# Turning x by a transfer, one state scaled by TensorE through diagonal matrices, and a new layout of the small stages

## The chip, the cores and the metric

The kernel runs on one core of a Trainium2 chip. The metric is the device time of one execution in microseconds (us), lower is better. TensorE is PE in the views, VectorE is DVE, ScalarE is ACT, GpSimd is POOL, SyncE is SP. PEld stands for TensorE's weight loads.

## The reference

32 sequences of 750 positions and 256 channels pass through three blocks. Cut to what is computed:

```python
# block 1: every second position, in segments of 128 positions
scores = einsum('bsqd,bskd->bsqk', x, x) / sqrt(256)
h = einsum('bsqk,bskd->bsqd', softmax(scores), x)
# block 2: h = h + mamba(layernorm(h))
x_in, z = split(xn @ W_in.T)                # 512 and 512 channels
u  = silu(conv4(x_in) + b_conv)
dt = softplus(u @ W_dt.T + b_dt); Bm = u @ W_B.T; Cm = u @ W_C.T   # 16 states
state = exp(dt * A) * state + (dt * u) * Bm ; y = sum over states of state * Cm
h = h + (y * silu(z)) @ W_out.T
# block 3: h = h + experts(layernorm(h)): 64 experts, the best 8 of each token,
#          256 places in each expert, silu(x Wg) * (x Wu) @ Wd, weighted and added
```

All of it is in float32.

## The kernel before

**Three phases.** The sequence phase works through blocks 1 and 2 and the routing of block 3, one sequence after the other. Then a short phase counts tokens by expert, and the expert phase gathers, multiplies and scatters. The change touches the sequence phase alone.

**A sequence's sixteen states.** Tokens of a sequence are 3 segments of 128. The recurrence runs state by state, `k` from 0 to 15, over 512 channels (4 chunks of 128 partitions) times 384 tokens. For each state the engines do this:

- ScalarE multiplies `dtu_t` (dt * u, tokens on the partitions) by the state's column of B in three operations (`scaled_dbu`, L380, into one of two buffers `dbu_t`), and makes `decay` with four exponentials (`decays`, L392, four buffers). It works two states ahead.
- TensorE turns `dbu_t` into `psB` with twelve transposes, in two pieces of 4 and 8 (`turn_dbu`, L932). `psB` exists once: a piece is overwritten when the scan of the state before has read it.
- VectorE runs the recurrence as two scans (`scan_piece`, L621), first 512 elements, then 1024, and signals `s_go` with a small instruction (L616).
- GpSimd multiplies by C (`times_c`, L360), when the next state's scan has begun.
- TensorE turns that product and adds it up in `psY`, three states later (`sum_y`, L944).

**The small stages.** All else of the sequence phase is cut into steps that are spread over the sixteen states, in the gaps around the recurrence: `body` of each engine lists at `if k == ...` what it does in a state. While sequence `b` is scanned, sequence `a = b + 2` is in its attention and first norm (`early`), `n = b + 1` in its projections, convolution, softplus and B and C (`front`), `m = b - 1` in its gate and output projection (`back`), `o = b - 2` in its second norm (`late`), and `c = b - 3` in its routing (`routed`). In a state TensorE does the first piece of `turn_dbu`, then `sum_y`, then the second piece, then its small stages. VectorE does its small stages first and then the two scans. ScalarE does a part of its small stages ahead of `scaled_dbu`, most between it and `decays`, and a few behind.

**Two banks.** The results of the small stages pass through two PSUM banks, `psM0` and `psM1`. `SLOTTED` names the products of each bank in the order in which they take it, and `LAG` says of which sequence each is at that time; a product can start when the one before it in its bank has been read. The names: `QT0`, `QT1` x turned, `S` the scores, `PT` probabilities turned, `AT0`, `AT1` the attention's output, `XN0`, `XN1` the normed input turned, `X0` to `X3` and `Z0` to `Z2` the input projections, `D0` to `D3` dt, `CB` B and C, `BT` B turned, `DU0` to `DU2` dt * u turned, `YT0` to `YT2` the gated y turned, `O0`, `O1` the output projection, `X2T0`, `X2T1` the second norm turned, `LG` the router's logits.

**Queues.** SP issues all transfers of this phase in a fixed order, each behind its wait: it stores a finished sequence, loads x (`load_x`, two transfers), stores and loads h, passes B and C through DRAM and spreads C over the partitions in four groups, and stores the routing.

**Carriers.** Where an instruction waits at a place that could also be reached with a register's value, the program before adds an increment of a semaphore `s_turn` that nobody reads; the wait then sits in a separate semaphore instruction ahead of the operation. On VectorE that holds for each first scan, for the aggregation of the norms' statistics (L653), and for the routing's MAX8 (L781, L803) and MATCH_REPLACE8 (L788, L816).

## Time and profile before

| | |
|---|---|
| median of 3 executions | 3411.68 us |
| lowest of the three | 3406.43 us |
| the profiled execution's own time | 3408.89 us |
| its span, first to last instruction | 3407.0 us |
| mean granted TensorE clock | 0.96 of full speed |
| busy over the span | TensorE 87%, VectorE 84%, ScalarE 83%, GpSimd 62% |
| first scan of a sequence begins | 71.31 us |

The third execution, at 6037.72 us, is far from the other two; the median is one of the two near ones. A profile shows one execution. Busy time counts an instruction from its start to its end, and neighbours on an engine overlap by up to a tenth of a microsecond, so what a step takes on an engine is better read from start to start. "Idle before" is the time in which the engine had nothing running, and the name behind it is who ended that. The steady part, from about 110 to 2760 us, repeats with each sequence.

### The profile page before, as it was taken

The page shows a single profiled execution, that of the slowest core. Times are in us where ns is not written, and L with a number is a line of the kernel's source. Part 1 is how long each engine was busy: PE and PEld are TensorE (multiplying, and loading weights), DVE is VectorE, ACT ScalarE, POOL GpSimd, SP SyncE. Part 2 cuts the span into 40 slices and gives each one's busy share as a digit, 9 for nine tenths or more (in the row PEclk, how much of TensorE's full clock was granted, in tenths as well). Part 3 has the DMA queues.
Part 4 walks back from the last instruction along what each step waited for, and adds up shares of the span by engine and source line. Part 5 has one row for each costly group of instructions (what it writes and reads, how often), then busy time and mean ns, then how long its engine had stood idle before and what let it go on. Part 6 is the DMA issues. An engine that isn't in the chain of part 4 may idle for free. (4 is left out here: it accounts for less than half of the span.)

```text
span 3407.0 us, 56637 instructions
## 1 busy us (share of the span) xinstructions
PE 2969.6 (87%) x19009; PEld 2397.3 (70%) x19009; DVE 2858.1 (84%) x4628; ACT 2823.4 (83%) x5457; POOL 2105.5 (62%) x780
## 2 busy tenths in 40 slices
PE   6899999999999999999999999999999987566664
PEld 4677777777777777777777777777777776455543
DVE  4888999999999999999999999999999997444442
ACT  5999999999999999999999999999999996211110
POOL 0666666666666666666666666666666665177776
PEclk8999999999999999999999999999999998588887
DMA  2111121212112111122222212112221111377774
GB/s 94 52 52 52 55 63 63 63 63 63 58 60 63 56 52 58 63 63 63 63 63 63 64 63 63 59 59 63 63 63 63 59 54 32 94 151 147 149 149 82
DMA packets 187455, 240.52 MB, mean 71 GB/s; under 512 B 45152, under 2 KB 165440, under 8 KB 187200
## 3 DMA queue, kind: packets, MB, share of 16 engines
q1 hardware_dynamic: 162624, 199.44, 18.7%
q0 software_dynamic: 24576, 37.77, 6.6%
q8 instruction: 149, 2.44, 0.3%
q14 instruction: 106, 0.87, 0.1%
HBM read 176.07 MB, written 61.08 MB: 70 GB/s over the span
## 5 line engine op out<-in xcount | busy, mean ns | idle before, releaser
L360 POOL TENSOR_TENSOR hid<-hid,c_all 128x1536 f32<-128x1536 f32 x512 | 1770.4, 3458 | 1100.4 <-DVEq L616 1094.9
L621 DVE TENSOR_TENSOR_SCAN hid<-decay,hid,psB 128x1024 f32<-128x1024 f32 x512 | 1201.4, 2347 | 88.7 <-PE psB L932 42.4
L392 ACT ACTIVATE decay<-dt,a_neg 128x383 f32<-128x383 f32 x2048 | 1086.4, 606 | 0.4
L380 ACT ACTIVATE dbu_t<-dtu_t,b_t 128x512 f32<-128x512 f32 x1536 | 993.2, 714 | 7.5 <-PE psB L932 7.4
L932 PE MATMUL psB<-ident,dbu_t 128*128 128x128 f32 x6144 | 856.5, 276 | 108.4 <-DVE hid L621 102.7
L932 PEld LDWEIGHTS psB<-ident,dbu_t 128*128 128x128 f32 x6144 | 699.0, 141 | 248.5 <-issue 122.7
L944 PE MATMUL psY<-ident,hid 128*128 128x128 f32 x6144 | 757.1, 273 | 1.7 <-POOL hid L360 1.7
L944 PEld LDWEIGHTS psY<-ident,hid 128*128 128x128 f32 x6144 | 689.7, 141 | 2.0 <-POOL hid L360 1.9
L621 DVE TENSOR_TENSOR_SCAN hid<-decay,psB 128x512 f32<-128x512 f32 x512 | 623.3, 1217 | 15.5 <-PE psB L932 10.7
L1019 PE MATMUL psM<-u,w_dt 128*128 128x384 f32 x1024 | 353.2, 488 | 3.4 <-ACT u L424 2.7
L1434 ACT ACTIVATE e_side<-e_psL,e_in_tile 128x128 f32<-128x128 f32 x128 | 45.8, 363 | 260.1 <-DVE e_in_tile L1558 259.4
L1019 PEld LDWEIGHTS psM<-u,w_dt 128*128 128x128 f32 x1024 | 185.0, 191 | 106.8 <-ACT u L424 2.9
L1407 POOL DMA_INDIRECT out_dram<-e_ys,e_dst_st x128 | 205.2, 1603 | 70.4 <-issue 59.3
L1009 PE MATMUL psM<-w_in,turned 128*128 128x512 f32 x384 | 181.4, 609 | 43.2 <-ACT zs_t L419 42.3
L721 DVE SCALAR_TENSOR_TENSOR u<-xin,w_cv,u 128x384 f32<-128x384 f32 x384 | 208.2, 610 | 8.4 <-ACT xin L412 7.2
L1001 PE MATMUL psM<-turned,w_in 128*128 128x384 f32 x512 | 183.2, 491 | 2.0 <-ACT xin L412 1.3
L1058 PE MATMUL psM<-w_out,yz 128*128 128x256 f32 x768 | 179.0, 384 | 0.7 <-issue 0.7
L1520 DVE COPY e_xt<-e_psG 128x512 f32<-128x512 f32 x64 | 44.3, 692 | 158.5 <-PE e_psG L1460 158.5
L1460 PE MATMUL e_psG<-e_ident,e_xg 128*128 128x128 f32 x256 | 50.6, 330 | 134.5 <-DMA e_xg<-x_weights_dram,e_src_st 134.3
L1398 POOL DMA_INDIRECT e_xg<-x_weights_dram,e_src_st x128 | 127.8, 998 | 49.2 <-issue 37.8
L1058 PEld LDWEIGHTS psM<-w_out,yz 128*128 128x128 f32 x768 | 143.0, 193 | 18.5 <-issue 1.1
L1009 PEld LDWEIGHTS psM<-w_in,turned 128*128 128x128 f32 x384 | 68.4, 191 | 114.0 <-issue 61.7
(148 smaller groups left out, 3294.3 us busy)
## 6 DMA issues: line engine op xcount, KB each, us to landing
c_all<-bc_rows_dram SPq DMA_DIRECT2D x128, 768.0 KB, 4.8
out_dram<-h SPq DMA_DIRECT2D x64, 384.0 KB, 5.6
h<-out_dram SPq DMA_DIRECT2D x32, 384.0 KB, 3.6
x_weights_dram<-normed SPq DMA_DIRECT2D x32, 384.0 KB, 2.6
xs<-in_x_dram SPq DMA_DIRECT2D x32, 256.0 KB
e_wg<-in_gate_dram SPq DMA_DIRECT2D x64, 128.0 KB, 2.7
e_wu<-in_up_dram SPq DMA_DIRECT2D x64, 128.0 KB, 3.0
e_wd<-in_down_dram SPq DMA_DIRECT2D x64, 128.0 KB, 3.4
```

The costliest lines, as they stand in the source:

```text
L360: nc.gpsimd.tensor_tensor(hid[k % 4][:, :, :], hid[k % 4][:, :, :], c_all[:, k, :].unsqueeze(1).to_broadcast([P, CH, L]), ALU.mult).then_i ...
L380: last = nc.scalar.activation(dbu_t[k % 2][:, t, :], dtu_t[q][:, t, :], ACT.Copy, scale=b_t[q][:, t, k:k + 1])
L392: last = nc.scalar.activation(decay[k % 4][:, c, 1:L], dt[q][:, c, 1:L], ACT.Exp, scale=a_neg[:, c, k:k + 1])
L621: nc.vector.tensor_tensor_scan(h[:, lo:hi], flat(decay[k % 4])[:, lo:hi], flat(psB)[:, lo:hi], h[:, lo - 1:lo] if j else 0.0, ALU.mult, AL ...
L721: last = nc.vector.scalar_tensor_tensor(out=u[:, c, :], in0=xin[:, c, t:t + L], scalar=w_cv[:, c, t:t + 1], in1=u[:, c, :], op0=ALU.mult, ...
L932: last = nc.tensor.transpose(flat(psB)[:, i * P:(i + 1) * P], dbu_t[k % 2][:, t, c * P:(c + 1) * P], ident[:, :])
L944: last = nc.tensor.matmul(psY[:, t, c * P:(c + 1) * P], hid[k % 4][:, c, t * P:(t + 1) * P], ident[:, :], is_transpose=True, start=(k == 0 ...
L1001: last = nc.tensor.matmul(psM[slot(name)][:, 0:L], w_in[:, k, c * P:(c + 1) * P], turned[:, k, :], start=(k == 0), stop=(k == KD - 1))
L1009: last = nc.tensor.matmul(psM[slot(name)][:, :], turned[:, k, t * P:(t + 1) * P], w_in[:, k, DI:2 * DI], start=(k == 0), stop=(k == KD - 1))
L1019: last = nc.tensor.matmul(psM[slot(name)][:, 0:L], w_dt[:, k, c * P:(c + 1) * P], u[:, k, :], start=(k == 0), stop=(k == CH - 1))
L1058: last = nc.tensor.matmul(psM[slot(name)][:, i * D:(i + 1) * D], yz[:, c, s * P:(s + 1) * P], w_out[:, c, :], start=(c == 0), stop=(c == C ...
L1407: nc.gpsimd.indirect_dma_start(out=h_out, out_offset=bass.IndirectOffsetOnAxis(ap=dst_st[q][:, h:h + 1], axis=0), in_=ys[q % 4][:, h, :], ...
```

## The change

**x turned by a transfer.** The host hands over a second, already turned copy of every second row of x, and `load_x` gets a third transfer, `xt`. The products `QT0` and `QT1` and their copies are gone; `scores` reads `xt`. The scale 1/16 was put into the copies as a factor of 1/4 on each side; now the exponential applies it, and the row's maximum is scaled by a second VectorE instruction.

**State 11 by diagonal matrices.** `DIAG` was empty and now holds 11. ScalarE skips `scaled_dbu` in that state. VectorE makes three 128x128 diagonal matrices of B's column in one operation (`spread_b`), and `turn_dbu` multiplies `dtu_t` by them, in place of turning `dbu_t`.

**Steps and banks.** The small stages stand in other states, and the products in another order and other banks. `XN1` is copied by ScalarE, no longer by VectorE. The increments of `s_turn` are gone. The loop over sequences on GpSimd is written out.

```diff
-DIAG = ()
+DIAG = (11,)
-SLOTTED = (("X0", "X2", "Z0", "Z2", "D0", "D1", "D2", "X2T0", "D3", "CB", "AT0", "YT0", "DU1", "O0", "XN1"),
-           ("O1", "X1", "X3", "Z1", "LG", "QT0", "QT1", "S", "PT", "X2T1", "BT", "AT1", "YT1", "DU0", "YT2",
-            "DU2", "XN0"))
+SLOTTED = (("X2T1", "X0", "X2", "Z0", "Z2", "D0", "YT0", "S", "PT", "AT0", "YT1", "DU0", "DU2", "XN0", "O1"),
+           ("XN1", "X1", "X3", "Z1", "LG", "D1", "X2T0", "D2", "D3", "CB", "AT1", "BT", "YT2", "DU1", "O0"))
...
             def load_x(a):
...
+                sp.dma_start(xt[:, :, 0:(S + DIL - 1) // DIL],
+                             w["x_t"][a].rearrange("(k p) t -> p k t", p=P)).then_inc(s_x, 16)
...
-            with pool.Fori(0, NB) as b:
+            for b in range(NB):
...
                     last = nc.scalar.activation(prob[:, s, :], psM[slot("S")][:, s * P:(s + 1) * P], ACT.Exp,
-                                                bias=nmax[:, s:s + 1],
+                                                bias=nmax[:, s:s + 1], scale=D ** -0.5,
...
             def row_max(a):
                 filled("S", a)
-                nc.vector.tensor_reduce(nmax[:, :], psM[slot("S")][:, 0:L].rearrange("p (s k) -> p s k", s=NSEG),
-                                        AX.X, ALU.max, negate=True).then_inc(s_nm, 1)
+                nc.vector.tensor_reduce(rmax[:, :], psM[slot("S")][:, 0:L].rearrange("p (s k) -> p s k", s=NSEG),
+                                        AX.X, ALU.max).then_inc(s_rm, 1)
+                dve.wait_ge(s_rm, a + 1)
+                nc.vector.tensor_scalar(nmax[:, :], rmax[:, :], -(D ** -0.5), None, ALU.mult).then_inc(s_nm, 1)
...
+            def spread_b(n, r):
+
+                dve.wait_ge(s_out[slot("BT")], number("BT", n))
+                for i, k in enumerate(DIAG):
+                    last = nc.vector.tensor_tensor(diag[:, i, :, :], ident[:, :].unsqueeze(1).to_broadcast([P, NSEG, P]),
+                                                   b_t[r][:, :, k:k + 1].to_broadcast([P, NSEG, P]), ALU.mult)
+                last.then_inc(s_dg, 1)
...
             def scores(b):
-                for name in last_of("QT0", "QT1"):
-                    copied(name, b)
+                pe.wait_ge(s_x, 48 * (b + 1))
                 emptied("S", b)
                 for s in range(NSEG):
                     for kd in range(KD):
-                        t = turned[:, kd, s * P:(s + 1) * P]
+                        t = xt[:, kd, s * P:(s + 1) * P]
```

The small stages by state, where they moved (TensorE: `D2` from state 7 to 8, `D3` from 8 to 9, `CB` from 9 to 10, `O1` from the next sequence's state 0 to 15, `X0`, `X1` and `X3` one state later, `Z0` and `Z1` from 3 to 4, `DU2` from 14 to 13, `YT0` from 11 to 6, `YT2` from 13 to 12, `BT` from 10 to between the pieces of 12, `XN1` from 15 to state 0 of the next, `X2T1` from 9 to state 0 one sequence later; VectorE: the routing's operations, before in states 6 to 9 with most of them in 7, over states 5 to 10, `finish_dt` of the first half from 9 to 10, its second half and both halves of `drive` from 10 to 11, the norm's statistics of h1 from 12 to 13, `norm` of h1 from 15 to 14).

TensorE, states 9 to 12 of a sequence, before. `xs` is x, `yz_t` the gated y, `bc_rows` B and C, `u` holds dt * u by then, and a number behind a name is its buffer.

```order
L932 MATMUL psB<-ident,dbu_t1 128x128 x8
L1028 MATMUL psM0<-u,w_bc 32x384 x4
L953 MATMUL psM1<-ident,normed2 128x128 x3
L932 MATMUL psB<-ident,dbu_t0 128x128 x4
L944 MATMUL psY<-ident,hid3 128x128 x12
L932 MATMUL psB<-ident,dbu_t0 128x128 x8
L1036 MATMUL psM1<-ident,bc_rows 128x128 x3
L988 MATMUL psM0<-xs,normed1 128x256 x2
L988 MATMUL psM1<-xs,normed1 128x256
L932 MATMUL psB<-ident,dbu_t1 128x128 x4
L944 MATMUL psY<-ident,hid0 128x128 x12
L932 MATMUL psB<-ident,dbu_t1 128x128 x8
```

And after the change, from the small stages of state 10 on:

```order
L1022 MATMUL psM1<-u,w_bc 32x384 x4
L982 MATMUL psM0<-xs,normed1 128x256 x2
L982 MATMUL psM1<-xs,normed1 128x256
L928 MATMUL psB<-diag,dtu_t1 128x128 x4
L943 MATMUL psY<-ident,hid0 128x128 x12
L928 MATMUL psB<-diag,dtu_t1 128x128 x8
L952 MATMUL psM0<-ident,yz_t 128x128 x4
L931 MATMUL psB<-ident,dbu_t0 128x128 x4
L943 MATMUL psY<-ident,hid1 128x128 x12
L1030 MATMUL psM1<-ident,bc_rows 128x128 x3
L931 MATMUL psB<-ident,dbu_t0 128x128 x8
```

The product of B and C (`u,w_bc`) moved one state back, in front of the attention's output and of the diagonal products of state 11.

ScalarE from state 9 to 11 before. `soft` is softplus, `normed1` holds the turned probabilities here.

```order
L430 ACTIVATE xin<-psM0,b_dt 128x384
L465 ACTIVATE normed1<-psM1 128x384
L438 ACTIVATE soft<-xin 128x768
L440 ACTIVATE soft<-soft 128x768
L442 ACTIVATE soft<-soft 128x768
L392 ACTIVATE decay2<-dt1,a_neg 128x383 x4
L380 ACTIVATE dbu_t1<-dtu_t1,b_t1 128x512 x3
L403 ACTIVATE turned2<-psM1 128x384
L447 ACTIVATE bc_rows<-psM0 32x384
L392 ACTIVATE decay3<-dt1,a_neg 128x383 x4
```

And now:

```order
L421 ACTIVATE xin<-psM1,b_dt 128x384
L456 ACTIVATE normed1<-psM0 128x384
L429 ACTIVATE soft<-xin 128x768
L431 ACTIVATE soft<-soft 128x768
L433 ACTIVATE soft<-soft 128x768
L438 ACTIVATE bc_rows<-psM1 32x384
L385 ACTIVATE decay3<-dt1,a_neg 128x383 x4
L373 ACTIVATE dbu_t0<-dtu_t1,b_t1 128x512 x3
```

The three scalings into `dbu_t1` of state 11 and the copy into `turned2` are no longer there, and the copy into `bc_rows` stands in ScalarE's state 9, while the product that it waits for stands in TensorE's state 10.

## Rows read from the trace of the kernel before

**Rows 1.** Windows: busy us of each engine, count, granted clock, DMA share, GB/s.
```profile
1000.00:1880.00 880.00, 821.90 (x5540) 668.35 (x5538) 832.22 (x1221) 853.59 (x1600) 552.56 (x161) 1.00 0.20 61
```
**Rows 2.** Waits of VectorE from 1000 to 1880 us: total us, times, longest.
```profile
DVE hid L621 <- PE psB L932: 9.8, 20, 0.7
DVE mv L653 <- DVE stat L648: 3.0, 20, 0.2
DVE nmax L643 <- PE psM L979: 2.5, 9, 0.3
...
DVE gleft L788 <- DVE gtop L784: 1.9, 10, 0.5
DVE top L803 <- DVE masked L797: 1.5, 10, 0.2
...
DVE hid L621 <- ACT decay L392: 0.4, 1, 0.4
```
**Rows 3.** Waits of ScalarE, same window; the longest of its three.
```profile
ACT denom L491 <- PE psM L1068: 10.4, 10, 1.0
```
**Rows 4.** Groups by line, 1000 to 1880 us: count, busy us, mean ns, idle before.
```profile
L380 ACT ACTIVATE dbu_t<-dtu_t,b_t 128x512 f32<-128x512 f32 x480 | 310.4, 714 | 0.0
...
L621 DVE TENSOR_TENSOR_SCAN hid<-decay,psB 128x512 f32<-128x512 f32 x160 | 194.8, 1217 | 1.1 <-issue 0.6 <-ACT decay L392 0.4
...
L403 ACT ACTIVATE turned<-psM 128x384 f32<-128x384 f32 x40 | 18.9, 472 | 0.0
...
L630 DVE COPY turned<-psM 128x384 f32<-128x384 f32 x20 | 10.0, 539 | 0.0
...
L751 DVE TENSOR_TENSOR biased<-score,bias 128x192 f32<-128x192 f32 x10 | 3.3, 334 | 0.0
...
L829 DVE TENSOR_SCALAR wsum<-wsum 128x3 f32<-128x3 f32 x10 | 1.7, 169 | 0.3
```
**Rows 5.** Timeline of states 13 to 15: start us, us, engine, line, count.
```profile
1551.24 1.22 DVE L621 TENSOR_TENSOR_SCAN hid<-decay,psB 128x512 f32<-128x512 f32 x1
...
1552.56 2.35 DVE L621 TENSOR_TENSOR_SCAN hid<-decay,hid,psB 128x1024 f32<-128x1024 f32 x1
...
1553.17 0.60 PE L932 MATMUL psB<-ident,dbu_t 128*128 128x128 f32 x4
...
1553.61 1.47 PE L944 MATMUL psY<-ident,hid 128*128 128x128 f32 x12
...
1554.83 1.22 DVE L621 TENSOR_TENSOR_SCAN hid<-decay,psB 128x512 f32<-128x512 f32 x1
...
1554.96 1.09 PE L932 MATMUL psB<-ident,dbu_t 128*128 128x128 f32 x8
...
1555.89 0.60 PE L953 MATMUL psM<-ident,u 128*128 128x128 f32 x4
...
1556.33 3.62 PE L1058 MATMUL psM<-w_out,yz 128*128 128x256 f32 x16
...
1559.79 0.60 PE L932 MATMUL psB<-ident,dbu_t 128*128 128x128 f32 x4
...
1561.02 1.22 DVE L621 TENSOR_TENSOR_SCAN hid<-decay,psB 128x512 f32<-128x512 f32 x1 [0.28 <-issue]
```
**Rows 6.** Timeline of VectorE, state 6.
```profile
1512.82 2.35 DVE L621 TENSOR_TENSOR_SCAN hid<-decay,hid,psB 128x1024 f32<-128x1024 f32 x1 [0.30 <-PE psB L932]
```
**Rows 7.** Timeline of TensorE, state 5 of the next sequence.
```profile
1595.09 0.49 PE L953 MATMUL psM<-ident,xs 128*128 128x128 f32 x3
...
1598.00 0.60 PE L932 MATMUL psB<-ident,dbu_t 128*128 128x128 f32 x4
```
**Rows 8.** Timeline of TensorE, the scores in state 7.
```profile
1522.13 1.50 PE L979 MATMUL psM<-turned 128*128 128x128 f32 x12
```
**Rows 9.** Timeline of TensorE at the start of the run.
```profile
5.58 0.87 PE L953 MATMUL psM<-ident,xs 128*128 128x128 f32 x3 [5.58 <-DMA xs<-in_x_dram]
...
8.74 2.90 PE L979 MATMUL psM<-turned 128*128 128x128 f32 x12 [0.67 <-ACT turned L403]
```

More of the change, by code:

```diff
@@ L214, in number @@
             ahead = [LAG[o] - LAG[name] + (i <= at) for i, o in enumerate(names)]
-            if not isinstance(batch, int):
-                return batch * len(names) + sum(ahead)
             return sum(min(max(batch + a, 0), NB) for a in ahead)
@@ L224, in each @@
         def each(eng, body):
-            def one(b, q):
-                fixed = isinstance(b, int)
-                body(b, q, scans=not fixed or 0 <= b < NB, back=not fixed or 0 <= b - 1 < NB,
-                     late=not fixed or 0 <= b - 2 < NB, routed=not fixed or 0 <= b - 3 < NB,
-                     front=not fixed or 0 <= b + 1 < NB, early=not fixed or 0 <= b + 2 < NB)
             for b in range(-2, NB + 3):
-                one(b, b % 2)
+                body(b, b % 2, scans=0 <= b < NB, back=0 <= b - 1 < NB, late=0 <= b - 2 < NB,
+                     routed=0 <= b - 3 < NB, front=0 <= b + 1 < NB, early=0 <= b + 2 < NB)
         block = ctx.enter_context(nc.Block())
@@ L241, in wait @@
                 after(sp, sem, count)
-                if not isinstance(count, int):
-                    sp.sem_inc(s_turn, 1)
             def load_x(a):
@@ L506, in body @@
                 for k in range(NS):
-                    if isinstance(b, int) and b == -1 and k == 0:
+                    if b == -1 and k == 0:
                         negated_a()
@@ L580, in body @@
                             copy_yz(m, 1)
-                    if k == 12:
                         if front:
-                            copy_dtu(n, r, 0)
-                        if back:
-                            copy_yz(m, 0)
-                    if k == 13:
-                        if front:
-                            copy_dtu(n, r, 2)
+                            copy_b(n, r)
                     if of:
                         decays(*of)
+                    if k == 2:
+                        if front:
+                            copy_xin(n, 3)
+                        if late:
+                            first_rstd(o, 1)
                     if k == 3:
@@ L594, in body @@
                             silu_z(n, r, 1)
+                    if k == 11:
+                        if front:
+                            copy_dtu(n, r, 0)
+                        if back:
+                            copy_yz(m, 2)
             each(act, body)
@@ L844, in body @@
                     if k == 0:
-                        if front:
-                            copy_turned("XN0", n, 0)
-                            copy_turned("XN1", n, 1)
+                        if late:
+                            add_block(o, 1)
                     if k == 1:
                         if late:
-                            add_block(o, 1)
                             second_stats(o)
@@ L889, in body @@
                             finish_dt(n, r, 1)
-                            drive(n, r, 1)
-                    if k == 11:
                         if early:
                             attended(a)
-                    if k == 12:
+                        if front:
+                            drive(n, r, 1)
+                    if k == 13:
                         if early:
                             first_stats(a)
+                    if k == 14:
+                        if early:
+                            newton(a, 0)
+                        if front:
+                            spread_b(n, r)
+                        if early:
+                            norm(a, 0, h1, normed1)
                     if k == 15:
                         if early:
-                            newton(a, 0)
-                            norm(a, 0, h1, normed1)
+                            copy_turned("XN0", a, 0)
                         if back:
@@ L954, in turn @@
                 last.then_inc(s_in[slot(name)], 1)
-            def turn_x(b, kd):
-                pe.wait_ge(s_x, 32 * (b + 1))
-                turn(f"QT{kd}", b, [xs[:, s, kd * P:(kd + 1) * P] for s in range(NSEG)])
             def turn_normed1(b, kd):
@@ L993, in project_xin @@
                 name = f"X{c}"
-                if isinstance(b, int) and b == 0:
+                if b == 0:
                     pe.wait_ge(s_w, 176)
@@ L1142, in body @@
                         if back:
-                            turn_yz(m, 0)
                             turn_yz(m, 1)
                     if k == 12:
+                        if back:
+                            turn_yz(m, 2)
                         if front:
@@ L1635 @@
         "x": as_is("x"),
+        "x_t": np.ascontiguousarray(np.asarray(inputs["x"])[:, ::DIL, :].transpose(0, 2, 1)),
         "in_t": turned("L0_attn_W_in"),
```

150 lines of the change are left out of this document (68 added, 82 removed).

## The prediction, as it was written before the result was known

> **What bounds it now.** I first ask how long a sequence takes. In the steady stretch the first scan ran 160 times in 880 us [rows 4], sixteen times in a sequence, so a sequence takes 88.0 us. 32 of them fill most of the run, and what the change does is done 31 times with all neighbours present; I count 31 periods. The expert phase is untouched.
>
> Next, who is busy. Over ten periods ScalarE was busy 853.6 us, VectorE 832.2, TensorE 821.9 [rows 1]: 97, 95 and 93%. By this view all three are full, and ScalarE first of all. So the third view decides, who waits for whom. VectorE's waits for another engine sum to 9.8 + 2.5 + 0.4 = 12.7 us in ten periods [rows 2], 1.27 us in a period. The rest of its idle time is its own: gaps behind its own results and between instructions. So 88.0 - 1.27 = **86.7 us of a period are VectorE's own work**, in its own order. It waited for a `decay` of ScalarE once in 160 states [rows 2]. ScalarE's 26.4 idle us in ten periods (880 - 853.6) are waits in small stages, the longest 10.4 for the router's logits [rows 3], not for room in the recurrence's buffers. The reader is to see a kernel that VectorE paces to within 1.5%, with ScalarE about 2.6 us a period behind it in load.
>
> **Where VectorE's 1.27 us come from.** The scans alone repeat after 1554.83 - 1551.24 = 3.59 us, the second one 1.32 us behind the first [rows 5]. On TensorE, from start to start, the first piece of `turn_dbu` takes 0.44 us, `sum_y` 1.35, the second piece 0.93 [rows 5]. The second piece of a state cannot start before the second scan of the state before has ended; it is done 1.06 us (0.13 + 0.93) after VectorE's next instruction begins. From there TensorE has its small stages, S, then 0.44 + 1.35 + 0.93 = 2.72 us, and must be through when VectorE wants the next state's second scan. With D(k) for VectorE's small work in state k, no wait arises if S(k) < 3.59 + 1.32 - 1.06 - 2.72 + D(k) + D(k+1) = 1.1 + D(k) + D(k+1). In state 14 before, S is 1559.79 - 1555.89 = 3.90, D(14) is nothing and D(15) at most 1561.02 - 1554.83 - 3.59 = 2.60 [rows 5]: 3.90 against 3.7, and 2.60 itself holds a gap of 0.28. In state 5 S is 1598.00 - 1595.09 = 2.91 [rows 7], state 6 has one short VectorE operation, and its second scan waited 0.30 [rows 6]. These are the two places a period that the 20 waits in ten periods name.
>
> **Part by part, a period.**
>
> *x by a transfer.* TensorE loses six transposes, 0.11 us each (0.44 / 4 [rows 5]): -0.66. ScalarE loses two copies of 472 ns [rows 4]: -0.94. SP gets one more issue and 384 KB; x is loaded in the second half of the period before the one that needs it, so I price the wait at nothing. If that cover went, the scores would wait, and behind them on TensorE the turning of state 8. VectorE gets one more dependent small operation: 169 ns and a 0.03 us gap, as L829 [rows 4]: +0.20.
>
> *State 11.* ScalarE loses three scalings of 714 ns that overlap; the busy time of the line is 310.4 / 160 = 1.94 us a state [rows 4]: -1.94. VectorE gets `spread_b`, two inputs and 384 elements. The trace has no such operation: L751 with 192 elements takes 334 ns, the copy of 384 elements 539 ns [rows 4]. I take 0.50, being nearer the one of its size, with 0.33 and 0.60 as ends. On TensorE twelve transposes become twelve real products. Six such products, the scores, are listed as twelve passes in 1.50 us [rows 8], where twelve transposes take 1.47 [rows 5]. So state 11 costs 3.0 in place of 1.5: +1.5. It lies in a state where VectorE now has the second half of softplus, the attention's output and both products dt * u ahead of its scan, over 4 us, so the test above holds with room; hidden. The Trainium skill (Perfetto Trace Analysis, § Transposes) says that logical transposes should use the transpose and not a standard matmul. The trace agrees on the price, twice the time for a block. Were TensorE the pace, the sum would grow by 1.5 - 0.66 = 0.84 us a period, 26 us in all.
>
> *`XN1` to ScalarE.* +0.47 there [rows 4]; on VectorE one of two copies goes, 0.46 from start to start (539 ns busy [rows 4]): -0.46. ScalarE in sum: -0.94 - 1.94 + 0.47 = **-2.4**.
>
> *Carriers.* VectorE's gaps ahead of the aggregations, the match and the second maximum are 3.0 + 1.9 + 1.5 us in ten periods [rows 2], 0.64 a period in four places, where an operation that waits within itself shows 0.03 (L829: 0.3 in ten [rows 4]). Between nothing and 0.5 is to be had; I take 0.40, as the nearest rows are those of the same engine with the wait inside. The carriers ahead of scans run while the engine is still busy and cost nothing.
>
> VectorE's own work: +0.20 + 0.50 - 0.46 - 0.40 = **-0.16** a period, ends -0.5 and +0.4.
>
> *Steps and banks.* I put the new states through the test. State 5 holds one dt product (2.91 - 0.33 = 2.58) and VectorE's D(5) and D(6) have grown by the routing that was heaped in state 7. State 14 holds 3.46 + 0.33, with the norm now in D(14): about 3.8 against 1.1 + 2.1 + 1.1. State 2 still holds two input projections ahead of a state without small work, and caused no wait before. All pass. So both waits should go. Small VectorE steps can wait anew: the first Newton step of h1 in state 14 comes less than 1 us behind ScalarE's root in its state 13, and `XN0`'s copy in 15 stands close behind the output projection. I leave 0.2 to 0.3 of the 1.27: **-1.0**, ends -1.27 and +0.1.
>
> *ScalarE's new wait.* It stands at the copy of B and C in its state 9 until TensorE has made them in state 10. By VectorE's work in these states I put this at some 2 us. Behind it are `decays` of state 11 and `scaled_dbu` of 12; state 11's scan comes after more than 4 us of VectorE's small work, so 3 to 4 us are left. Its total waits may rise from 2.6 to 86.6 - 83.0 = 3.6 us without touching the end.
>
> *Start.* The scores need no turned x: they could begin when x is there, about 5.6 to 6.5 us, not at 8.7 [rows 9]; the QT steps are gone from the second sequence's start too, and one bank wait of the dt products. I take -5, ends 0 and -8. GpSimd's written-out loop: nothing, it waits for VectorE anyway.
>
> **Sum.** A period -0.16 - 1.0 = -1.16, times 31 = -36; with the start -41. The profiled execution took 3408.9, which gives 3368; the median of the runs is 2.8 above it: **3370 us**, 1.2% less.
>
> **Rivals.**
>
> 1. *The wait comes back elsewhere* (chance 0.18). For it: all three engines are over 93% full, and a new order of 60 steps meets new bank waits. Against: the test above passes in every state. A period stays near 88: 3395 to 3412, about 3405.
>
> 2. *ScalarE is the pace* (0.10). It has the highest busy share [rows 1]. Then its 2.4 us count in full: 31 x 2.4 = 74, with the start 79: 3333. The Trainium skill (Perfetto Trace Analysis, § Identifying the Most-Contended Engine) calls the engine with the highest occupancy the one to optimize first, which points here. Against it: VectorE waited for `decay` once in ten periods [rows 2]. A floor stands in the way too: with no wait left and my best own work, a period is 86.7 - 0.5 = 86.2, and 31 x 1.8 + 8 = 64 gives 3348.
>
> 3. *Slower: ScalarE waits for B and C and never catches up* (0.07). Mechanism: the copy in state 9 stands behind TensorE's state 10, which VectorE's scans gate, while `decays` and `scaled_dbu` queue behind the copy. It decides once ScalarE's waits pass 3.6 us a period. With 7.5 us, twice my count, a period is 83.0 + 7.5 = 90.5, 31 x 2.5 = 78: 3490.
>
> 4. *TensorE is the pace* (0.03): +26, 3438 at most.
>
> The forecast itself gets 0.62, its own range 3345 to 3395. The range that should hold the time in 8 of 10 cases takes in rivals 1 and 2: 3333 to 3415. What a measurement of this kernel can tell from no change I set at 2%, 68 us: faster than 3343 has 0.10 (rival 2 and an edge of the forecast, less what the floor forbids), slower than 3480 has 0.05, the rest 0.85.
>
> **What would show it.** A first scan 160 times in about 868 us; ScalarE's busy time near 830 in ten periods and its idle time grown, led by a wait of the copy into `bc_rows` for the product of B and C; VectorE's waits for `psB` near nothing; the twelve diagonal passes at about twice a transpose; the gaps ahead of L653's and L803's successors near 0.03. The forecast is wrong if VectorE's waits for others stay at 1 us, or if it waits for `decay` or `psB` behind a late ScalarE.

## The result

The changed kernel takes **3321.99 us** (median of 4, 3318.74 to 3324.03), the kernel before beside it 3409.05: ratio 0.975, 95% interval 0.9731 to 0.9769, 2.5% less time. I had forecast 3370 with a range of 3333 to 3415. The direction was right, the size was not: the time lies below the whole range. One execution of before, at 6037.72 us, is far from all others and is left out of the ratio; without it the median of before is 3406.43. So the change gave 84 to 87 us, where I had forecast 41 (3370 against the 3411.68 that I had then).

Both profiled executions stand close to their medians: 3408.89 us before, 3318.74 after, -90.2. Three stretches split them, read from the first and last start of the first scan: before 71.3 and 2864.5 us (span 3407.0), after:

```profile
L606 DVE TENSOR_TENSOR_SCAN hid<-decay,psB x512: 1212/1218/1223, 66.6 to 2781.1; 128x512 f32<-128x512 f32 x171
```

So the start gave 4.7 us (forecast 5), the scanned part 2793.2 - 2714.5 = **78.7**, and what follows the last scan 6.6 (span 3317.0). The last figure I don't lean on: two profiles of the changed kernel differ by 4 us there. In the middle, from state 0 to state 0, a sequence takes **85.50 us** in place of 88.07 (mean of 23): **-2.57 us a period** where I had forecast -1.16.

### The profile page after: what moved, and what is told of

Its sections match the earlier page's. It is cut to its first block and busy times, and to the rows that moved or that the text cites. A ratio compares the mean times of both kernels' runs of the same rounds, so it can differ in the third digit from the quotient of the medians.

```text
span 3317.0 us, 55585 instructions
## 1 busy us (share of the span) xinstructions
PE 2970.5 (90%) x19201; PEld 2422.1 (73%) x19201; DVE 2834.6 (85%) x4661; ACT 2750.8 (83%) x5329; POOL 2106.7 (64%) x780
## 5 line engine op out<-in xcount | busy, mean ns | idle before, releaser
L373 ACT ACTIVATE dbu_t<-dtu_t,b_t 128x512 f32<-128x512 f32 x1440 | 931.1, 713 | 11.0 <-PE psB L931 8.7
L931 PE MATMUL psB<-ident,dbu_t 128*128 128x128 f32 x5760 | 803.0, 276 | 75.6 <-DVE hid L606 70.5
L931 PEld LDWEIGHTS psB<-ident,dbu_t 128*128 128x128 f32 x5760 | 652.9, 141 | 191.4 <-DVE hid L606 75.7
```

The source lines that it names most:

```text
L373: last = nc.scalar.activation(dbu_t[k % 2][:, t, :], dtu_t[q][:, t, :], ACT.Copy, scale=b_t[q][:, t, k:k + 1])
L931: last = nc.tensor.transpose(flat(psB)[:, i * P:(i + 1) * P], dbu_t[k % 2][:, t, c * P:(c + 1) * P], ident[:, :])
```

## The profile after

The window of [rows 1], after. It holds 880 / 85.5 = 10.3 periods, not 10.0:

```profile
1000.00:1880.00 880.00, 847.74 (x5754) 695.46 (x5752) 849.59 (x1260) 856.10 (x1607) 569.27 (x165) 1.00 0.22 68
```

ScalarE is still the busiest by share, with 856.1 / 10.3 = 83.2 us a period (forecast 83.0). The granted clock is 1.00, TensorE's 2.4 GHz level, as in [rows 1]. The waits of VectorE (total us in the window, times, longest) answer to [rows 2]:

```profile
DVE hid L606 <- PE psB L931: 4.1, 12, 0.4
DVE h L674 <- DVE rinv L668: 2.0, 10, 0.2
...
DVE hid L606 <- DVE hid L606: 0.9, 2, 0.5
```

Waits for another engine fell from 12.7 us in ten periods to 4.1 in 10.3, from 1.27 to 0.40 a period: -0.87, where I had -1.0. The gaps of the aggregation, MATCH_REPLACE8 and MAX8 are gone from the list. ScalarE, beside [rows 3]:

```profile
ACT denom L482 <- PE psM L1062: 10.4, 10, 1.0
ACT bc_rows L438 <- PE psM L1022: 9.9, 10, 1.0
ACT dbu_t L373 <- PE psB L931: 1.0, 4, 0.3
```

The new wait for B and C is there at half the forecast length, 1.0 us. The groups by line, beside [rows 4]:

```profile
L928 PE MATMUL psB<-diag,dtu_t 128*128 128x128 f32 x240 | 30.0, 275 | 0.0
L373 ACT ACTIVATE dbu_t<-dtu_t,b_t 128x512 f32<-128x512 f32 x464 | 300.1, 713 | 1.0 <-PE psB L931 1.0
L716 DVE TENSOR_TENSOR diag<-ident,b_t 128x384 f32<-128x384 f32 x10 | 5.5, 550 | 0.0
L615 DVE COPY turned<-psM 128x384 f32<-128x384 f32 x10 | 5.3, 533 | 0.0
```

The diagonal products take 3.0 us a period, as priced. The matrices take VectorE 0.55 us of busy time, and 0.47 from start to start. VectorE in state 14, beside [rows 5]:

```profile
1504.57 0.16 DVE L649 SCALAR_TENSOR_TENSOR nw<-nw,rs 128x3 f32<-128x3 f32 x1
1504.77 0.16 DVE L652 SCALAR_TENSOR_TENSOR rstd<-nw,rs 128x3 f32<-128x3 f32 x1
1504.85 0.55 DVE L716 TENSOR_TENSOR diag<-ident,b_t 128x384 f32<-128x384 f32 x1
1505.31 1.05 DVE L662 TENSOR_SCALAR normed<-h,mv,rstd 128x256 f32<-128x256 f32 x3
```

These four rows hold what I had missed. The last Newton step (`rstd`) needs the one before it and starts 0.20 us after the start of that one. The diagonal matrices need neither, and start 0.08 us after the start of a step that itself lasts 0.16. The lists of waits don't show this, since the gap at each place is 0.04 us; it must be read **from start to start**.

At the start the scores (L973) begin at 6.69 us, not at 8.74 [rows 9]:

```profile
6.69 2.90 PE L973 MATMUL psM<-xt 128*128 128x128 f32 x12 [6.69 <-DMA xs<-in_x_dram]
```

## The experiments

Four reasons could stand behind the missing 1.4 us. **Theory A**: VectorE paces, as forecast, and its own work shrank far more than I had priced, by carriers and by the new order of operations within a state. **Rival B**: the carriers ahead of scans. **Rival C**: banks and steps, by waits alone. **Rival D**: ScalarE paced, and its relief by 2.4 us made the gain. All runs, with the mean period of each profile (sequences 5 to 28). The effects are mostly under 1% of the time, so each is held against the changed kernel's own repeats: 3318.74 to 3324.03 us and, in e15, 3312.28 to 3325.04, with periods of 85.50 and 85.48.

| run | us | ratio to before, 95% | period |
|---|---|---|---|
| the change | 3321.99 | 0.975, 0.9731 to 0.9769 | 85.50 |
| e1 carriers ahead of scans back | 3332.56 | 0.9794, 0.9778 to 0.9811 | 85.90 |
| e2 the other carriers back | 3335.35 | 0.9801, 0.9785 to 0.9818 | 85.92 |
| e3 dependent steps back to back | 3341.48 | 0.9818, 0.9802 to 0.9835 | 86.07 |
| e4 state 11 by ScalarE | 3341.74 | 0.9817, 0.9801 to 0.9834 | 86.26 |
| e5 before, no carriers | 3393.78 | 0.9971, 0.9959 to 0.9982 | 87.80 |
| e6 before, x by transfer | 3393.84 | 0.9968, 0.9956 to 0.9981 | 87.80 |
| e7 before, state 11 diagonal | 3404.16 | 1.0002, 0.9993 to 1.0012 | 88.09 |
| e8 change with e1, e2, e3 | 3366.79 | 0.9897, 0.988 to 0.9914 | 86.98 |
| e9 diagonals on GpSimd | 3321.71 | 0.9762, 0.9746 to 0.9778 | 85.51 |
| e10 steps between scans | 3332.47 | 0.9799, 0.9758 to 0.9841 | 85.41 |
| e11 all separated | 3743.94 | 1.0993, 1.0975 to 1.1011 | 100.05 |
| e12 e9, one state later | 3319.09 | 0.9759, 0.9734 to 0.9784 | 85.48 |
| e13 free steps between scans | 3321.78 | 0.9771, 0.9751 to 0.9791 | 85.67 |
| e14 e12 and e13 | 3319.99 | 0.9763, 0.9742 to 0.9783 | 85.64 |
| e15 the change again | 3320.72 | 0.9768, 0.9747 to 0.9788 | 85.48 |
| e16 ScalarE's waits out | 3318.78 | 0.9751, 0.9735 to 0.9767 | 85.49 |
| e17 e14 and e16 | 3314.44 | 0.9739, 0.9722 to 0.9755 | 85.39 |
| e18 before, e5 to e7 together | 3378.05 | 0.9928, 0.9912 to 0.9945 | 87.36 |

### e1 to e3: what the change took off VectorE

e1, the carrier ahead of a first scan:

```diff
                 if j == 0:
+                    dve.sem_inc(s_turn, 1)
                     nc.vector.engine_nop().then_inc(s_go, 1)
```

> The changed kernel, with a carrier (the separate semaphore instruction that takes the wait) back ahead of each first scan. The changed kernel took 3322 us, a period 85.50 us from first scan to first scan. Theory A (VectorE paces; these carriers run while its engine is still busy, as the forecast said): no change, 85.5 us a period, 3317 to 3328 us, and a pure scan-to-scan step stays at 3.59 us. Rival B (a carrier costs 0.05 us wherever it stands, and the 0.85 us a period that the scans lost came from there): +0.8 us a period, about 3347 us.

Measured: +0.40 us a period, between the two. The step from scan to scan stayed at 3.59 us, as A says, but at four of the sixteen scans the operation ahead is short. One of them, in the changed kernel first and in e1 then:

```profile
1036.60 0.18 DVE L768 TENSOR_TENSOR gsum<-best 128x24 f32<-128x24 f32 x1
1036.74 1.22 DVE L606 TENSOR_TENSOR_SCAN hid<-decay,psB 128x512 f32<-128x512 f32 x1
```

```profile
1040.52 0.18 DVE L771 TENSOR_TENSOR gsum<-best 128x24 f32<-128x24 f32 x1
1040.78 1.22 DVE L609 TENSOR_TENSOR_SCAN hid<-decay,psB 128x512 f32<-128x512 f32 x1
```

0.14 us from start to start became 0.26. In the mean this place costs 0.14 us a period, the comparison of the groups 0.14, and the two aggregations 0.11 together: all of the 0.40 but 0.01 to 0.02. The forecast's sentence that carriers ahead of scans "run while the engine is still busy and cost nothing" holds behind a long operation, not behind a short one.

e2, at the aggregations, MAX8 and MATCH_REPLACE8 (one place shown):

```diff
                 dve.wait_ge(s_st[j], n + 1)
+                dve.sem_inc(s_turn, 1)
                 for s in range(NSEG):
                     last = nc.vector.bn_aggr(mv[j][:, s, :], stat[j][:, s, :])
```

> The changed kernel, with the carriers back ahead of the two aggregations, MAX8 (twice) and MATCH_REPLACE8 (twice). Theory A (each leaves the engine empty for longer, because nothing of it is issued ahead): +0.55 us a period, read from the steps from start to start of before and after (aggregation 0.26, fill ahead of the match 0.13, MAX8 0.13, the rest), so 86.05 us a period and about 3340 us with the end. The forecast's term was 0.40 a period: 3334. Rival C (the gain is all banks and steps, so carriers don't matter): 3322.

Measured: +0.42 us a period. The 0.55 that I expected of this run was too much; the forecast's 0.40 was sized rightly, and read from the right rows. From start to start the four places that it named cost 0.46, and the first MAX8 and the second MATCH_REPLACE8, which stand right behind a scan here, nothing.

e3, the order alone (two of its four places):

```diff
                             newton(o, 1)
-                        if routed:
-                            score_experts(c)
-                        if late:
                             norm(o, 1, h2, normed2)
                         if routed:
+                            score_experts(c)
                             pair_experts(c)
...
                             newton(a, 0)
-                        if front:
-                            spread_b(n, r)
-                        if early:
                             norm(a, 0, h1, normed1)
+                        if front:
+                            spread_b(n, r)
```

> The changed kernel with VectorE's independent operations no longer between dependent ones: Newton, norm, then the router's score; Newton, norm, then the diagonal matrices; both products dt * u together, then the attention's output; the last two convolution operations in the old order. The same operations stand in the same states. Theory A (a dependent operation starts about 0.12 us later after its predecessor than an independent one does, and VectorE paces): +0.4 to 0.5 us a period (Newton 0.24, finish of dt 0.16, convolution 0.1), about 3336 us. Rival C (order within a state costs nothing, banks and steps are all): 3322 within 5.

Measured: +0.57 us a period, 20 us, by nothing but who stands behind whom. In e3's trace:

```profile
1084.65 0.16 DVE L652 SCALAR_TENSOR_TENSOR rstd<-nw,rs 128x3 f32<-128x3 f32 x1
1084.85 1.06 DVE L662 TENSOR_SCALAR normed<-h,mv,rstd 128x256 f32<-128x256 f32 x3
```

0.20 us between starts, where the changed kernel has 0.08. Newton's last steps account for 0.24, the finish of dt 0.19, convolution 0.13, the router's score 0.11. That is 0.67 of VectorE's own work; some 0.1 of it went into a wait for `psB` that was there. Rival C falls, as order within a state is worth something. One of the places is not an order of the kernel before: there the router's score stood alone in state 6, with a scan behind it, and took 0.16 us. The change's own gain by order is the other three, 0.55.

### e4: what state 11 is worth

```diff
-DIAG = (11,)
+DIAG = ()
...
-                        if front:
-                            spread_b(n, r)
```

> The changed kernel with state 11 scaled by ScalarE again: no diagonal matrices, no diagonal products. ScalarE gets 1.94 us a period more, VectorE loses an operation of 0.47 us from start to start, TensorE 1.5 us. Theory A (VectorE paces): between -15 us (VectorE's 0.47 us times 31) and +5 us, since ScalarE's 83.2 us of work a period grow to 85.1 and leave it no slack; 3307 to 3327 us. Rival D (ScalarE paced before, and its relief made the gain): +1.94 us times 31, about 3380 us.

Measured: +0.76 us a period, 3341.74 us. Both fall short: a loss, where A allowed at most 5 us, and far less than D's 1.94. The step from scan 10 to scan 11 alone grew from 7.73 to 8.50 us in the mean, by all of the 0.76. There VectorE's dt * u overwrites `u` and waits until TensorE has read it for B and C:

```profile
DVE u L731 <- PE psM L1020: 6.3, 10, 0.8
```

ScalarE's scaling for state 11 stands right ahead of its copy of `D3`; B and C take the same bank after `D3`. With 1.94 us more there, all of it comes late. So ScalarE counts where its work stands ahead of a product that VectorE needs, and not by its sum. The matrices that VectorE no longer makes in state 14 gave nothing: 0.12 of their 0.47 went into Newton's last step, which now stands behind the one it needs, the rest into waits for `psB` in states 15 and 0. e12 meets the same.

### e5 to e7 and e18: the parts, put into the kernel before

e5 takes VectorE's six `sem_inc(s_turn, 1)` out, with no other edit.

> The kernel before with VectorE's carriers gone and nothing else changed (before took 3404 us beside the first four). From e1 and e2 I now hold: a carrier costs about 0.10 to 0.14 us where the operation ahead of it on VectorE is short, also ahead of a scan, and nothing behind a long one. In the kernel before such places are the two aggregations, MAX8 and MATCH_REPLACE8 (0.42 us a period in e2) and two or three scans behind short operations (0.40 in e1). Theory A: up to 0.8 us a period, 25 us, less what VectorE then waits more for psB, as both tight states are still there: 0.5 to 0.8, 3378 to 3388. The forecast's term, 0.40: 3391. Rival C (banks and steps only): 3404.

Measured: 3393.78 us, -0.26 a period, short of A's 3378 to 3388. From start to start VectorE's own work fell by 0.79: 0.49 at the four places that the forecast had counted, 0.10 at the first MAX8, and 0.20 at the two scans behind an aggregation. 0.53 came back as waits. The timeline of VectorE names a new one:

```profile
1431.16 0.56 DVE L642 TENSOR_REDUCE nmax<-psM 128x3 f32<-128x384 f32 x1 [0.80 <-PE psM L973]
...
1469.88 2.35 DVE L620 TENSOR_TENSOR_SCAN hid<-decay,hid,psB 128x1024 f32<-128x1024 f32 x1 [0.72 <-PE psB L926]
```

The scores now come 0.8 us late for their row maximum, and state 15's second scan waits as before. So in the old order TensorE took back two thirds of what the removal gave.

e6 has the `xt` transfer, the exponential's factor and the second operation of `row_max`, and drops `QT0` and `QT1`, as in the change's diff.

> The kernel before with x turned by the transfer alone: QT0, QT1 and their copies gone, the row's maximum scaled by a second VectorE operation, all else in its old state and bank. TensorE -0.66 us a period, ScalarE -0.94, VectorE +0.17 (start to start, as measured in the changed kernel). Theory A: the start -5, VectorE's own +0.17 x 31 = +5, state 5's wait of 0.3 us gone, -9: 3395. Rival D (ScalarE's load counts for half or more, as the 0.77 of 1.94 + 0.47 in e4 suggests): another -0.4 us a period, 3383.

Measured: 3393.84 us, -0.27 a period, as theory A had it (3395). VectorE's `row_max` +0.22, its waits -0.5.

e7 has `DIAG = (11,)` and, in VectorE's body:

```diff
+                    if k == 14:
+                        if front:
+                            spread_b(n, r)
```

> The kernel before with state 11 by diagonal matrices alone; VectorE makes them in its state 14, where it has no other small stage. ScalarE -1.94 us a period, VectorE +0.47 of work in a state where it waited up to 0.9 us for psB, TensorE +1.5. Theory A (VectorE paces, its 1.27 us of waits a period come from TensorE's small stages and not from ScalarE): 0 to +0.3 us a period, 3404 to 3413. Rival D (ScalarE is close behind, and part of the psB waits are its lateness): -0.5 to -0.8 us a period, 3380 to 3390.

Measured: nothing, 1.0002. ScalarE lost 1.94 us a period and used them to wait:

```profile
ACT dbu_t L380 <- PE psB L940: 12.8, 10, 1.6
```

In the kernel before ScalarE had room; rival D falls for it. Of VectorE's 0.46 us in state 14, 0.33 went into the wait for `psB` that stood behind it in state 15.

e18 is the three together, with the old steps and banks.

> The kernel before with the change's parts but for steps and banks: x by the transfer, state 11 by diagonal matrices, no carriers on VectorE; XN1 is still copied by VectorE. Alone these gave -0.27 (e6), 0.0 (e7) and -0.26 us (e5) a period. Theory E (ScalarE and VectorE were level before, too, so each relief alone was lost to the other): together more than their sum of 0.53: VectorE's own 86.8 - 0.79 + 0.22 + 0.46 = 86.7 and what is left of the psB waits, 0 to 0.4: -1.0 to -1.4 us a period, 3361 to 3373. Rival C (the parts just add up, the rest is banks and steps): 3404 - 17 = 3387.

Measured: 3378.05 us, -0.71 a period: more than the sum, 0.53, and less than theory E's 1.0. Neither was right. Of the 2.57, then, 0.71 come from these three parts alone, and 1.86 from the rest: the new steps, order and banks, and `XN1`'s copy by ScalarE, which is 0.47 of VectorE's work.

### e8: does it add up to the forecast?

> The changed kernel with all VectorE carriers back and the order within the states of e3. Alone these cost 11 (e1), 14 (e2) and 20 us (e3) over the changed kernel's 3321. Theory A (all three are VectorE's own time, and VectorE paces): they add up to 45, about 3366 us, 86.9 us a period; that is what the forecast said for the change, whose sum had none of e1 and e3 in it. Rival (another engine takes over within that much, or they share a cause): less than 35, under 3356.

Measured: 3366.79 us and 86.98 us a period. The three add up: 0.40 + 0.42 + 0.57 = 1.39 singly, 1.48 together. That 3367 lies so near the forecast's 3370 is in part luck, and the expectation above claims too much: e8 also takes back the carriers for which the forecast had counted 0.40. Without that term the forecast would have been 3370 + 0.40 x 31 = 3382, so e8 is some 15 us, or 0.5 us a period, faster than what is left of the forecast. No run isolates these 0.5 us.

### e9 to e11: VectorE's operations beside GpSimd's

e9:

```diff
                 for k in range(NS):
                     times_c(b, k)
+                    if k == 12 and b + 1 < NB:
+                        spread_b(b + 1, (b + 1) % 2)
```

> The changed kernel with the diagonal matrices made by GpSimd, behind its multiplication of state 12, and no longer by VectorE. VectorE loses 0.47 us a period, nothing else changes but GpSimd, which is busy for 569 of 880 us. Theory A (VectorE paces the changed kernel): -0.47 x 31 = -15 us, 3307. Rival D (ScalarE, with 83.2 us of busy time and 2 us of waits in 85.5 us, is as much the pace by now, as e4 showed from the other side): no gain, 3317 to 3325.

Measured: no gain, as rival D had it. But the trace shows no wait for ScalarE. It shows this, of GpSimd and VectorE in state 14:

```profile
994.51 0.83 POOL L361 TENSOR_TENSOR diag<-ident,b_t 128x384 f32<-128x384 f32 x1
...
994.61 0.76 DVE L660 SCALAR_TENSOR_TENSOR nw<-nw,rs 128x3 f32<-128x3 f32 x1
```

An operation on three elements, 0.16 us elsewhere, takes 0.76 and ends at 995.37, GpSimd's at 995.34. That is 0.60 us a period lost on VectorE for 0.47 gained.

e10 moves the two additions of h, the second aggregation and the gate's last third between the scans:

```diff
-                        for j in range(PB):
-                            scan_piece(b, k, j)
+                        scan_piece(b, k, 0)
+                    for step in between:
+                        step()
+                    if scans:
+                        scan_piece(b, k, 1)
```

> The changed kernel with five small VectorE steps moved between the two scans of their state: both parts of the addition of h, the aggregation of the second norm, and the last third of the gate (four states: 0, 1, 2 and 15). In the changed kernel a scan starts 0.104 us after the end of the first scan it builds on, but 0.08 us ahead of the end of an independent operation, so 0.19 us a state stand between two scans. Theory A: 4 x 0.19 and 0.12 for the aggregation off its statistics, 0.88 us a period, -27 us: 3295. Rival: the second scan comes later by the step's length, TensorE's second piece and all behind it too, and VectorE waits for psB in the next state: 3322 or more.

Measured: 85.41 us a period, and runs from 3319 to 3348, too scattered for a verdict. The gaps between the scans fell by 0.75 us a period, as said, but VectorE's waits rose from 0.39 to 1.00, as the rival had it: for `psB` 0.52 at state 0's second scan (0.35 in the changed kernel) and 0.30 at state 7's (none there), and 0.16 for the router's logits.

e11 does so for thirteen states, routing dealt out over states 5 to 12.

> The changed kernel with e9 and e10 in it, and VectorE's steps of thirteen states dealt out so that nearly every operation stands behind an independent one: routing from state 5 to 12, one step of each state between the scans. Theory A alone: 13 x 0.19 = 2.5 us, some 12 dependent pairs of 0.117 = 1.4, and 0.47 of e9: 4.4 us a period less, 81.1, if VectorE still paced. It can't: ScalarE is busy for 83.2 us a period and waits for 2. So theory A with ScalarE as the next bound: 84 to 85 us a period, 3275 to 3307. Rival (the later second scans and the later routing make waits that eat it): 3322 or more.

Measured: 3743.94 us. The miss is large, and has the cause of e9. GpSimd's multiplication starts with the first scan, and an operation between the scans meets it:

```profile
1068.61 3.45 POOL L353 TENSOR_TENSOR hid<-hid,c_all 128x1536 f32<-128x1536 f32 x1 [2.81 <-DVEq L612]
...
1069.50 2.62 DVE L820 TENSOR_TENSOR masked<-masked 128x48 f32<-128x48 f32 x1
```

It ends at 1072.12, the multiplication at 1072.06. With such operations VectorE's busy time grew from 82.5 to 99.2 us a period, and the period by 14.5. The scans, with one input in PSUM, keep their 1.22 and 2.35 us. Operations that read PSUM, the aggregation and MAX8 keep their times, too. The Trainium skill (SBUF — State Buffer, § Who interferes with whom) says that VectorE and GpSimd share a pair of ports under an exclusive lock, and that a VectorE instruction with two SBUF inputs contends there with a GpSimd instruction that reads SBUF. The two pairs of rows agree: both operations have two inputs in SBUF and end within 0.03 and 0.06 us of GpSimd's. Two inputs are not the only case, though: `wsum<-wsum`, with one input and three elements, lasted 2.58 us in e11 and 0.17 in the changed kernel.

### e12 to e17: where the next bound lies

e12 is e9 with `k == 13`.

> As e9, but GpSimd makes the diagonal matrices behind its multiplication of state 13, so that they fall on the copy and the addition of state 15, which read PSUM. In e9 they fell on the Newton steps of state 14, one of which took 0.76 us in place of 0.16 and ended with them. Theory A' (VectorE paces, and e9 lost its gain because an operation with two SBUF inputs waits until GpSimd is done): -0.47 us a period, 3307 us. Rival D (ScalarE is the pace, e9 would have gained nothing anyway): 3317 to 3325.

Measured: Newton's step is back at 0.16 us, and there is still no gain: 85.48. VectorE's wait for `psB` grew from 4.1 to 8.8 us in the window, at two places:

```profile
1428.69 2.35 DVE L617 TENSOR_TENSOR_SCAN hid<-decay,hid,psB 128x1024 f32<-128x1024 f32 x1 [0.25 <-PE psB L932]
1433.04 2.35 DVE L617 TENSOR_TENSOR_SCAN hid<-decay,hid,psB 128x1024 f32<-128x1024 f32 x1 [0.55 <-PE psB L932]
```

These are the second scans of states 15 and 0, behind the output projection. The 0.47 us in state 14 were its cover, D(14) in the prediction's test. VectorE's own work fell by 0.35 us and its waits grew by 0.45. So e12 speaks neither for A' nor for D: what ends last at this place is TensorE's work, and less work on VectorE doesn't move it.

e13 moves the second aggregation, the gate's last third, both MATCH_REPLACE8 and the second MAX8 between the scans of states 1, 2, 7, 8 and 9.

> The changed kernel with five steps between the two scans of their state that e11's trace shows undisturbed there by GpSimd's multiplication: the second norm's aggregation, the last third of the gate, both MATCH_REPLACE8 and the second MAX8. Theory A': 5 x 0.19, and four dependent pairs broken (0.117 each), 1.4 us a period less of VectorE's own work; ScalarE's 83.2 us and its waits leave room for about that: 84.1 us a period, 3278; with 0.3 us of new waits 3288. Rival D: 3317 or more.

Measured: 3321.78 us, 85.67 a period. VectorE is ahead earlier, and waits where there was no wait:

```profile
DVE hid L606 <- PE psB L957: 10.3, 30, 0.4
DVE hid L606 <- ACT decay L385: 9.4, 10, 1.0
```

0.6 us a period for `psB` in state 7, and 0.95 for `decay` of state 9: there ScalarE is the bound.

e14 is e12 and e13 together.

> e12 and e13 together. VectorE's own work 85.5 - 0.47 - 1.4 = 83.6 us a period, ScalarE's busy time 83.2: the two are level, so waits must come. Theory A': 84.0 to 84.5 us, 3275 to 3290. Rival D: 3317 or more.

Measured: 3319.99 us, 85.64 a period: again no gain.

e15 is the changed kernel once more, with no edit.

> The changed kernel once more, as the yardstick beside e12 to e14: 3318 to 3325 us, 85.5 us a period.

Measured: 3320.72 us and 85.48; e9 and e12 to e14 differ from it by less than their intervals.

e16:

```diff
-                        if routed:
-                            tanh_logits(c)
                         if front:
                             silu_z(n, r, 2)
+                        if routed:
+                            tanh_logits(c)
+                        if front:
                             silu_u(n)
...
                             softplus(n, 1)
+                        if of:
+                            decays(*of, range(0, CH // 2))
+                        if front:
                             copy_bc(n)
```

> The changed kernel with ScalarE's two fixed waits taken out by order alone: the router's tanh goes behind the scaling of z's last part (it waited 1.0 us for the logits), and the copy of B and C behind the first two of state 11's four exponentials (it waited 1.0 us). No work is added or removed. Theory E (after e9 and e12 to e14: ScalarE, 83.2 us busy and 2.0 us in these two waits, and VectorE, some 85.1 us, are level): ScalarE gets 1.5 us of slack, VectorE then paces alone: -0.1 to -0.4 us a period, 3308 to 3318. Theory D (ScalarE alone paces): -1.5 x 31, about 3275. Theory A (VectorE alone): 3321.

Measured: 85.49, no gain. The two waits are halved, and ScalarE waits for `psB`, that is behind VectorE, instead:

```profile
ACT denom L483 <- PE psM L1067: 5.6, 10, 0.6
ACT bc_rows L439 <- PE psM L1027: 4.8, 10, 0.5
ACT dbu_t L373 <- PE psB L936: 4.4, 12, 0.4
```

So rival D falls for the changed kernel, too: room for ScalarE alone gives nothing, as A says.

e17 is e14 and e16 together.

> e14 and e16 together: VectorE without the diagonal matrices and with five steps between the scans, ScalarE without its two waits. e14 alone gained nothing (3320 beside 3321). Theory E (two engines level, each hides what is taken off the other): VectorE 83.6 us of own work and 0.4 to 0.8 of waits, ScalarE 83.8: 84.0 to 84.6 us a period, 3275 to 3295. Theory A and theory D alone: the same as e16, or the same as e14.

Measured: 3314.44 us, 85.39. Theory E's 3275 to 3295 was too good: against the changed kernel VectorE has 1.7 us a period less of own work and 1.6 more of waits. With ScalarE's waits halved, VectorE's wait for `decay` halved too (9.5 us in the window in e14, 4.7 here), which gave 0.25 us a period against e14. Of the two it is the wait for the logits that stands ahead of that `decay` in ScalarE's order; no run takes out one alone. `psB` stayed at 14.9. It is the fastest version, 0.2% under the change by the medians, with overlapping intervals: no gain that I can claim.

## Why the forecast was wrong in size

- **Held.** VectorE paces: what was added to it came out in full or nearly so (e1, e2, e3, e8). Taking work off it gave nothing where it was another engine's cover (e4, e12). Start, 4.7 us for 5. `XN1` -0.47 for -0.46, the matrices +0.47 for +0.50, the row's maximum +0.17 for +0.20, TensorE's diagonal products 3.0 for 3.0, waits -0.87 for -1.0, ScalarE's load 83.2 for 83.0. No run isolates the written-out loop on GpSimd.
- **The step that failed** is "VectorE's own work: +0.20 + 0.50 - 0.46 - 0.40 = -0.16 a period". It fell by 2.57 - 0.87 = 1.70. The mechanism was right, and two terms were missing or too small. First, carriers were counted at 0.40 in four places. Put back into the changed kernel they cost 0.82 (e1, e2), and out of the kernel before they took 0.79 off VectorE's own work (e5); what the forecast put at nothing were scans behind short operations, and it left out the first MAX8. Second, it moved operations to new neighbours at no price: an operation right behind the one it needs starts about 0.12 us later than it would behind another. That is 0.55 in the three places where the change parts such a pair within a state (e3). -0.87 - 0.82 - 0.55 - 0.47 + 0.47 + 0.17 is -2.07; the other 0.50 no run isolates. Start-to-start times put 0.21 us at the addition of h, 0.11 at the norm and 0.1 (carriers as in e1 and e2) to 0.25 (as in e5) at routing, whose steps now stand in states 5 to 10, with scans between them.
- **What the list of moves didn't show.** The list ahead of the prediction names states, not the order within one. It also leaves out that the second part of the addition of h moved from state 1 to state 0, so that a scan parts it from the statistics that read it.
- **The test looks at one state at a time.** It passes for state 15 (small stages of 1.7 us against 2.5), and yet 0.35 of the 0.39 us of waits that are left a period stand at state 0's second scan:

```profile
1080.34 2.35 DVE L606 TENSOR_TENSOR_SCAN hid<-decay,hid,psB 128x1024 f32<-128x1024 f32 x1
1083.73 1.04 PE L931 MATMUL psB<-ident,dbu_t 128*128 128x128 f32 x8
...
1088.08 1.04 PE L931 MATMUL psB<-ident,dbu_t 128*128 128x128 f32 x8
...
1089.15 2.35 DVE L606 TENSOR_TENSOR_SCAN hid<-decay,hid,psB 128x1024 f32<-128x1024 f32 x1 [0.37 <-PE psB L931]
```

  The test assumes that a second piece starts when the second scan of the state before ends. State 14's ended at 1082.69, but TensorE was still behind with the output projection and began state 15's piece at 1083.73; the delay ran on into state 0.
- **The floor** of 86.2 us and 3348, on which I cut the lower chances, was built on the same sum: my "86.7 us of VectorE's own work" were a property of the order, and the order is what the change rewrote.
- **Rival 2** gave 3333, nearest to the result, by the wrong mechanism, so its nearness is luck: ScalarE's relief gave nothing in the kernel before (e7), and more room nothing after (e16). The Trainium skill's rule to optimize the engine with the highest occupancy first (Perfetto Trace Analysis, § Identifying the Most-Contended Engine) would have led there. By busy share ScalarE leads in both kernels, 97% of the window; in neither did its relief alone save time.
- **What stays open.** e4 shows that ScalarE is no bystander in the changed kernel, e13 that it is the bound at state 9 once VectorE gains. Which wait would have to go after e17 to get under 85.4 us was not tried.

## What to carry over

Where one engine paces a program of many short operations, price each one from the start of one to the start of the next, and sort the pairs by whether the second needs the first; a new order is a change of work. A step off the pacing engine is worth its time only if it wasn't the cover of another engine's stretch: ask in each state which engine comes next, within half a microsecond. And before putting work on GpSimd, or a VectorE operation beside it, look where their inputs lie.

## What the hardware did that I had not expected

- On VectorE an operation that needs the one before starts about 0.035 us after its end, an independent one 0.08 us before its end (0.16 us steps, start to start 0.20 and 0.08); a second scan that continues the first starts 0.10 us after its end.
- A carrier costs 0.10 to 0.14 us behind most short operations (0.03 and 0.08 behind the two aggregations in e1) and nothing behind a long one (scan to scan 3.59 us with and without, e1).
- VectorE operations of 0.16 to 0.2 us lasted up to 2.6 us beside GpSimd's multiplication (e11). Nothing is reported as a wait: the row only gets longer, and VectorE's busy time rises.
